# A table of places for the shared units of a decoder layer, a projection row one slot earlier, and the residual rows' fetches elsewhere in SP's queue

## The reference

```python
def attn(h):                                   # causal self attention
    q, k, v = split(h @ W_attn + b_attn, 3)    # to 16 heads
    q, k = _layernorm(q, q_gamma, q_beta), _layernorm(k, k_gamma, k_beta)
    p = softmax(where(causal, q @ k.T * 32 ** -0.5, min))
    return (p @ v) @ W_proj + b_proj
def xattn(x, ctx):                             # cross attention, top 32 of 512 keys
    Q, K, V = x @ Wq.T + bq, ctx @ Wk.T + bk, ctx @ Wv.T + bv
    s, i = top_k(Q @ K.T / sqrt(32), 32)
    return (softmax(s) @ V[i]) @ Wo.T + bo
def ffn(x):                                    # width 2048, quantized
    gate = silu(_bitlinear(x, w_gate)); up = _bitlinear(x, w_up)
    return _bitlinear(gate * up, w_down)
x = x + attn(_layernorm(x))
x = x + xattn(_layernorm(x), ctx)
x = x + ffn(_layernorm(x))
```

## Time and profile before

| | us |
|---|---|
| median of three executions | 3904.87 (3895.12 to 3911.36) |
| the profiled execution | 3917.24 |
| its span | 3915.5 |
| busy in it: PE, DVE, ACT, POOL | 3310.2, 3220.0, 2451.7, 1917.9 |
| first cross slot starts, last cross slot starts | 490.7, 3749.1 |
| mean granted clock of PE | 0.867 |

### The profile page before, as it was taken

The page is one execution under the profiler, slowest core; times in us unless marked ns, Lnnn a source line. Parts: engine busy times, 40 slices in busy tenths (PEclk is TensorE's granted clock), DMA queues, the critical chain, the costliest instruction groups (busy, mean ns, idle before and its releaser), DMA issues.

```text
span 3915.5 us, 61337 instructions
## 1 busy us (share of the span) xinstructions
PE 3310.2 (85%) x18502; PEld 2433.7 (62%) x18502; DVE 3220.0 (82%) x7571; ACT 2451.7 (63%) x4921; POOL 1917.9 (49%) x2444
## 2 busy tenths in 40 slices
PE   1577888999989998999999989999899988877765
PEld 1355567766666676667667667667666766554542
DVE  4311189999989999899989998999989998999961
ACT  2344466676777677667766677767666776555533
POOL 0122334446555466546654655546554654355445
PEclk7677878898999989988989999988998898887768
DMA  8112232232223222322223222322233221211100
GB/s 279 46 49 65 80 84 73 74 82 75 51 76 88 75 69 79 84 79 74 76 72 84 75 52 74 87 76 67 79 88 83 65 71 41 62 46 36 33 22 19
DMA packets 167443, 283.04 MB, mean 72 GB/s; under 512 B 40639, under 2 KB 52939, under 8 KB 166606
## 3 DMA queue, kind: packets, MB, share of 16 engines
q1 hardware_dynamic: 160782, 275.98, 25.9%
q10 hardware_dynamic: 6336, 3.15, 0.3%
HBM read 113.27 MB, written 31.46 MB: 37 GB/s over the span
## 4 chain that ended last, share of the span: by engine, by line
DVE 33%; PE 32%; POOL 11%; issue 8%; ACT 6%; SPq 4%; DMA 1%; DVEq 0%; POOLq 0%; ACTq 0%
DVE cW L881 15%; DVE top L876 12%; PE bank L682 6%; PE bank L607 6%; PE bank L654 5%; SPq L513 4%; PE bank L593 3%; PE bank L670 2%; PE bank L701 2%; PE bank L635 2%; POOL hh L1111 2%; POOL srs L1147 2%; POOL hh L1115 2%; PE bank L694 2%; DVE smx L1013 2%
## 5 line engine op out<-in xcount | busy, mean ns | idle before, releaser
L881 DVE MATCH_REPLACE8 cW<-top,cW 128x512 f32<-128x512 f32 x1536 | 1026.3, 676 | 0.0
L876 DVE MAX8 top<-cW 128x8 f32<-128x512 f32 x1536 | 980.7, 680 | 0.0
L1168 POOL TENSOR_TENSOR cS<-cS,cW 128x512 f32<-128x512 f32 x512 | 642.2, 1276 | 233.2 <-ACT cW L825 232.7
L797 ACT ACTIVATE PT<-bank 128x512 f32<-128x512 f32 (+3 forms) x1024 | 538.0, 525 | 314.4 <-PE bank L593 310.6
L607 PE MATMUL bank<-cv,PT 128*128 128x33 f32 x4096 | 586.0, 290 | 121.8 <-ACT PT L797 120.6
L607 PEld LDWEIGHTS bank<-cv,PT 128*128 128x128 f32 x4096 | 555.0, 210 | 157.0 <-ACT PT L797 151.0
L1175 POOL TENSOR_SCALAR cnb<-top 128x2 f32<-128x2 f32 x256 | 49.3, 193 | 871.6 <-DVE top L876 857.9
L607 PEld LDWEIGHTS bank<-sv,PT 128*128 128x128 f32 x2560 | 398.7, 211 | 77.7 <-ACT PT L797 55.4
L825 ACT ACTIVATE cW<-cW,cnb 128x512 f32<-128x512 f32 x512 | 347.8, 734 | 127.6 <-DVE cW L881 127.2
L819 ACT ACTIVATE cS<-cS,cnb 128x512 f32<-128x512 f32 x512 | 380.1, 742 | 46.9 <-POOL cnb L1175 24.0
L682 PE MATMUL bank<-w_group,xT 128*128 128x384 f32 x1024 | 403.3, 541 | 0.0
(11 more groups left out here) (151 smaller groups left out, 6131.8 us busy)
## 6 DMA issues: line engine op xcount, KB each, us to landing
sk_stack<-part SPq DMA_DIRECT2D x512, 64.0 KB, 2.0
sq_stack<-part SPq DMA_DIRECT2D x512, 64.0 KB, 2.0
ck_stack<-part SPq DMA_DIRECT2D x512, 64.0 KB, 2.0
cq_stack<-part SPq DMA_DIRECT2D x512, 64.0 KB, 2.0
w_group<-wa_by_group SPq DMA_DIRECT2D x32, 768.0 KB, 4.8
w_group<-wc_by_group SPq DMA_DIRECT2D x32, 768.0 KB, 4.3
feed<-in_x SPq DMA_DIRECT2D x32, 256.0 KB, 3.0
feed<-in_ctx SPq DMA_DIRECT2D x32, 256.0 KB, 3.0
```

Of the source, the lines that this page charges most:

```text
L797: act.activation(PT[k][:, 0:n], turned_ps[k][:, 0:n], ACT.Copy).then_inc(turned_read, step("turned_read", label))
L876: dve.max(top8[:, j, r, :], src[:]).then_inc(topk, step("topk", (c, r, "max", j)))
L881: dve.match_replace(cW[j][:], top8[:, j, r, :], src[:], REPLACED).then_inc(topk, step("topk", (c, r, "replace", j)))
L1168: pool.tensor_tensor(cS[m % 2][j][:], cS[m % 2][j][:], cW[j][:], ALU.subtract).then_inc(cprob, step("cprob", (m, j)))
```

## The change

`schedule(b)` is a table for each batch b of the slots, counted from the batch's first cross slot, in which its shared units stand, in place of the rule "three slots a tile". `cross_rows` move from 15, 16, 17, 18 to 15, 17, 18, 19. The 16 chunks of the MLP's gate and up stand in 20 to 33, ten early and six late; `hT` in 22, 25, 30, 35 (places 6, 9, 14, 3) and `down`, now apart, in 23, 25, 30, 37 (places 7, 9, 14, 5). The last two batches keep three slots a tile, the last but one three slots later. `self_qkv` row 0 moves to cell 5 of the slot before (q = 3), row 1 from cell 3 to 2, row 2 from 6 to 5, row 3 from cell 1 to 3. `self_out` moves from cell 3 to 4 where q = 2, and DVE's `self_rows` behind ROUND_1 of the second half. POOL's `inner_quant` also follows an early last chunk. On SP the residual rows' DMAs move from ahead of the weights and copies of a slot to behind them, and the fetches of `x1res`, `x2res` and `xres` are those of the next slot.

```diff
+def schedule(b):
+
+    def dense(first):
+        chunks = [(first + 3 * t + r, early) for t in range(NT) for r in range(2) for early in (True, False)]
+        ends = tuple(first + 3 * t + 2 for t in range(NT))
+        return chunks, ends, ends
+    if b == NB - 1:
+        return ((15, 16, 17, 18), *dense(17))
+    if b == NB - 2:
+        return ((15, 17, 18, 19), *dense(20))
+    chunks = [(20, True), (20, False), (21, True), (21, False), (22, False), (23, True), (24, True), (24, False),
+              (25, False), (26, True), (27, True), (29, True), (31, True), (32, True), (32, False), (33, True)]
+    return (15, 17, 18, 19), chunks, (22, 25, 30, 35), (23, 25, 30, 36 if b == NB - 3 else 37)
+
+
+def planned(s, part, entry, tiles=NT):
+
+    out = []
+    for b in range(NB):
+        for i, at in enumerate(schedule(b)[part]):
+            if at == entry(s - LAG - SLOTS * b):
+                out.append(tiles * b + i)
+    return out
+
+
 def cross_tile(s):
-    return tile_at(s, LAG + 15)
+    return next(iter(planned(s, 0, lambda at: at)), None)
 
 
 def x2_tile(s):
-    return tile_at(s, LAG + 16)
+    return cross_tile(s - 1)
...
 def mlp_chunk(s, early):
 
-    t, r = mlp_step(s)
-    return [(t, 2 * r + (not early))] if t is not None and r < 2 else []
+    return [divmod(i, NF) for i in planned(s, 1, lambda at: (at, early), NT * NF)]
+
+
+def mlp_inner(s):
+    return planned(s, 2, lambda at: at)
 
 
 def mlp_down(s):
-    t, r = mlp_step(s)
-    return [t] if t is not None and r == 2 else []
+    return planned(s, 3, lambda at: at)
 
 
 def cells(s):
 
     u = [[] for _ in range(CELLS)]
-    g, q = self_group(s), s % NT
+    q = s % NT
+    g = s // NT + 2
+    if q == 3 and 0 <= g < NGROUPS:
+        u[5].append(("self_qkv", g, 0))
+    g = self_group(s)
     if g is not None:
-        for at, cell, unit in ((0, 0, ("self_qkv", g, 0)), (0, 3, ("self_qkv", g, 1)), (0, 6, ("self_qkv", g, 2)),
-                               (1, 1, ("self_qkv", g, 3)), (3, 2, ("self_kT", g)), (3, 3, ("self_qT", g))):
+        for at, cell, unit in ((0, 2, ("self_qkv", g, 1)), (0, 5, ("self_qkv", g, 2)),
+                               (1, 3, ("self_qkv", g, 3)), (3, 2, ("self_kT", g)), (3, 3, ("self_qT", g))):
             if at == q:
                 u[cell].append(unit)
...
     if self_tile(s) is not None:
         u[2].append(("self_oT", self_tile(s)))
-        u[3].append(("self_out", self_tile(s)))
+        u[4 if q == 2 else 3].append(("self_out", self_tile(s)))
     if x2_tile(s) is not None:
         u[4].append(("x2T", x2_tile(s)))
+    for t in mlp_inner(s):
+        for n in range(NF):
+            u[3 + n].append(("hT", t, n))
     for early, cell in ((True, 2), (False, 6)):
         for t, n in mlp_chunk(s, early):
             u[cell] += [("gate", t, n), ("up", t, n)]
     for t in mlp_down(s):
-        for n in range(NF):
-            u[3 + n].append(("hT", t, n))
         u[7].append(("down", t))
     for k, f in enumerate(feeds(s)):
         u[5 + k].append(("feed", *f))
...
-                for t in mlp_down(s - 1):
-                    C.plan("h_dve", ("out", t))
                 for early, at in ((False, s - 1), (True, s)):
+                    for t in mlp_down(s - 1) if early else ():
+                        C.plan("h_dve", ("out", t))
...
                         done += len(feeds(s - 1))
                         while pending and ring[pending[0]] - RING < done:
                             load_feed(pending.pop(0))
-                        t = x1_tile(s)
-                        if t is not None:
-                            sp.wait_ge(x1_stats, upto("x1_stats", ("x1", t)))
-                            sp.dma_start(rows(x1_rows, t), xres[:]).then_inc(x1_out, step("x1_out", t, 16))
-                        t = x2_tile(s)
-                        if t is not None:
-                            sp.wait_ge(dve_rows, upto("dve_rows", ("x2", t)))
-                            sp.dma_start(rows(x2_rows, t), x2t[:]).then_inc(x2_out, step("x2_out", t, 16))
-                        t = cross_tile(s)
-                        if t is not None:
-                            if t:
-                                sp.wait_ge(dve_rows, upto("dve_rows", ("x2", t - 1)))
-                            sp.wait_ge(x1_out, upto("x1_out", t, 16))
-                            sp.dma_start(x1res[:], rows(x1_rows, t)).then_inc(x1res_in, step("x1res_in", t, 16))
-                        t = self_tile(s)
-                        if t is not None:
-                            if t:
-                                sp.wait_ge(x1_out, upto("x1_out", t - 1, 16))
-                                sp.wait_ge(x1_norm, upto("x1_norm", (t - 1, 4)))
-                            sp.dma_start(xres[:], rows(x_rows, t)).then_inc(xres_in, step("xres_in", t, 16))
-                        for t in mlp_down(s):
-                            sp.wait_ge(x2_out, upto("x2_out", t, 16))
-                            if t:
-                                sp.wait_ge(y_out, upto("y_out", t - 1, 16))
-                            sp.dma_start(x2res[:], rows(x2_rows, t)).then_inc(x2res_in, step("x2res_in", t, 16))
                         for at, which, g, before in loads:
                             if at == s:
                                 load_weights(which, g, before)
@@ -554,8 +554,33 @@
                             for unit, j in ((k_unit, 0), (k_unit, 1), (q_unit, 0), (q_unit, 1),
                                             (k_unit, 2), (q_unit, 2), (k_unit, 3), (q_unit, 3)):
                                 copy_part(unit, j)
+                        t = cross_tile(s)
+                        if t is not None:
+                            sp.wait_ge(dve_rows, upto("dve_rows", ("x2", t)))
+                            sp.dma_start(rows(x2_rows, t), x2t[:]).then_inc(x2_out, step("x2_out", t, 16))
+                        t = cross_tile(s + 1)
+                        if t is not None:
+                            if t:
+                                sp.wait_ge(dve_rows, upto("dve_rows", ("x2", t - 1)))
+                            sp.wait_ge(x1_out, upto("x1_out", t, 16))
+                            sp.dma_start(x1res[:], rows(x1_rows, t)).then_inc(x1res_in, step("x1res_in", t, 16))
+                        t = self_tile(s)
+                        if t is not None:
+                            sp.wait_ge(x1_stats, upto("x1_stats", ("x1", t)))
+                            sp.dma_start(rows(x1_rows, t), xres[:]).then_inc(x1_out, step("x1_out", t, 16))
                         for t in mlp_down(s - 1):
                             store_y(t)
+                        for t in mlp_down(s + 1):
+                            sp.wait_ge(x2_out, upto("x2_out", t, 16))
+                            if t:
+                                sp.wait_ge(y_out, upto("y_out", t - 1, 16))
+                            sp.dma_start(x2res[:], rows(x2_rows, t)).then_inc(x2res_in, step("x2res_in", t, 16))
+                        t = self_tile(s + 1)
+                        if t is not None:
+                            if t:
+                                sp.wait_ge(x1_out, upto("x1_out", t - 1, 16))
+                                sp.wait_ge(x1_norm, upto("x1_norm", (t - 1, 4)))
+                            sp.dma_start(xres[:], rows(x_rows, t)).then_inc(xres_in, step("xres_in", t, 16))
...
                         top(c, 0, ROUND_3)
                         top(c, 1, FIRST_MAX)
                         self_maxima(s, 0)
+                        top(c, 1, ROUND_1)
                         self_rows(s)
-                        top(c, 1, ROUND_1)
                         feed_stats_of(s + 1)
                         top(c, 1, ROUND_2)
                         mlp(s, True)
...
                     def inner_quant(s):
-                        for t, n in mlp_chunk(s, False):
+                        for t, n in mlp_chunk(s, True) + mlp_chunk(s, False):
                             if n == NF - 1:
```

More of the change, by code:

```diff
@@ L99, in cross_group @@
     return g if 0 <= g < NGROUPS else None
-def mlp_step(s):
-    b, at = divmod(s - (LAG + 17), SLOTS)
-    t, r = divmod(at, 3)
-    return (NT * b + t, r) if 0 <= b < NB and t < NT else (None, None)
 def mlp_chunk(s, early):
-    t, r = mlp_step(s)
-    return [(t, 2 * r + (not early))] if t is not None and r < 2 else []
+    return [divmod(i, NF) for i in planned(s, 1, lambda at: (at, early), NT * NF)]
+def mlp_inner(s):
+    return planned(s, 2, lambda at: at)
 def mlp_down(s):
-    t, r = mlp_step(s)
-    return [t] if t is not None and r == 2 else []
+    return planned(s, 3, lambda at: at)
 def cells(s):
     u = [[] for _ in range(CELLS)]
-    g, q = self_group(s), s % NT
+    q = s % NT
[3 more added lines that the diff above has]
+    g = self_group(s)
     if g is not None:
-        for at, cell, unit in ((0, 0, ("self_qkv", g, 0)), (0, 3, ("self_qkv", g, 1)), (0, 6, ("self_qkv", g, 2)),
```

(3 more changed lines are left out.)

## The result

The changed kernel took 3968.45 us (median of four, 3959.18 to 3971.99) against 3905.38 for the kernel before on the same chip: ratio 1.016 [1.013, 1.019], 63 us slower where I had forecast 40 faster.

A forecast was written before the change was run, and what follows sets the result against it. DVE and PE were both near full, so only DVE's idle time could return: -4.4 us a batch, six times -26, with -14 before the cross units, total -40, giving a median of 3865 us; range 3805 to 3925.

The forecast's parts named there:

- the early part: Before the cross units start: row 0 fills PE's 4.16 us wait for the copies; -3.6 us a group, four groups, -14.
- place 12: Batch place losing a projection row, `down` and four hT units, over 8 us of PE work; DVE's idle time put at 0.5.
- place 13: Batch place where PE, now early, waits for DVE's norms before `self_oT`; DVE's idle time put at 1.5, from 3.5.
- The weight load of q = 1: Places 1 and 5: row 3 in cell 3 delays the load for `cross_v`; PE waits 2.1 us, DVE pays 0.
- my other bound: Places 1 and 5: upper bound on DVE's cost from the late weight load, 3 us each, against 0 taken.
- Place 9: The wait for POOL's quantized `hh` covers PE's wait for the q = 1 weight load; idle time put at 1.0.
- the sum for place 10: Idle 8.8 + 1.4 + 1.8 - 2.5, less 2, gives 7.5; 5.5 once place 9's POOL wait and half clock fall away.
- The residual rows: Fetches a slot ahead but behind the copies: `x1res` comes no earlier in place 15, whose idle time goes 2.7 to 4.0.
- 3 by its fetch: Place 3 had no own term, being among eight places going 6.2 to 3.6; the prediction's wording is "0 by its fetch".
- Place 7's load: `w_group` lands near 2362.7 for row 0 in cell 5; PE waits 9 us, place 8 goes from 0.6 to 7.3.
- the first rival: Load not exposed: `w_group` lands before PE asks, or PE is late anyway; place 8 keeps 0.6; 3836 us, chance 0.26.
- the last rival: Half clock behind the gaps: place 8 waits 12, places 1 and 5 cost 3 each; 3929 us, chance 0.15.

## Why the prediction was wrong

Of the gains that the steps named, three came: the early part 18.0 us (predicted 14), place 12 at 0.3, place 13 at 1.5. PE waits for the load in places 7, 1 and 5. The terms below were wrong; together they are the 15.1 us a batch between 24.9 and 40.0.

*The weight load of q = 1 (the step that failed).* I had PE wait 2.1 us in places 1 and 5, and put DVE's cost at 0 since "PE's load in both slots is 3 us under DVE's". The wait was 3.0 and 2.4 us on average. The cost is not the wait but what stands behind it: `cross_v` took 8.3 us for its four eights of matmuls instead of 4.6, and what PE had in hand was spent. Place 2 paid 4.8 us more than I said; leaving out the load took it to 0.2. Even my other bound, 3 each, was short of place 2. I had the engines' loads about right (PE 20.55 us busy in place 1 against DVE's 24.74), and that was no cover. Nor does the length of the wait give the price: the 2.4 us in place 5 cost DVE only some 0.5 us, in place 6 (1.1 against 0.6 with the row in cell 1). Why place 5 is so cheap was not tested.

*Place 9, in the same step.* I wrote that there the wait for POOL covers the load. The runs show the reverse: that the row leaves cell 1 opens a gap of 1.14 us, the row runs at half clock and releases the load later, and both meet in place 10 (the run with the row in cell 2 parts the two). It idled 10.9 us, not 5.5, and 36 of the 58 us vanish when row 3 is back in cell 1 at places 9 and 13 alone. In the sum for place 10 I had counted the fall of the wait for POOL as a gain, to 5.5; with row 3 back in cell 1 the place idles 5.3, so that part of the sum holds.

*The residual rows.* I saw the fetch behind the copies and priced it in place 15 only (4.0; it was 6.2). The same order at place 3, a tile that the table itself puts there, I gave 0 ("3 by its fetch"). It idled 4.4 us, and 7.1 in the run with row 3 in cell 1, where PE was not late. Here the prediction missed the largest gain as well: the two DMAs ahead of the copies are worth 50 us by the ratios with the old rows.

*Place 7's load.* I said PE waits 9 us and place 8 takes 7.3; it waited 3.8 in the row above, and place 8 idled 3.0. Its load landed 7.8 us after its issue at most, but the row was reached late, at 2808.1, for PE had waited 3.86 us a batch for ACT in front of it: the first rival's argument. Place 7 itself stayed at 4.5 us where I took 1.2. The run with the table alone has 3.8 there, 3.4 of it DVE's maxima waiting for POOL's product `hh`: I put it down to the late chunk that the table sets in place 6, and didn't test it.

So the last rival came true in kind, half clock behind the gaps, at places 1 and 9, hardly at 5; place 8, where it put 12 us, idled 3.0. It gave 3929 where 3968 was measured, since it had neither place 9 nor place 3. The trace had its sign already in the earlier trace rows: a gap of 2.85 us and 0.50 behind it. The Trainium skill's section "HAM oscillation — how this bites in real kernels" of "TensorE: Matmul & The Clock Gate" says that PE is re-throttled by a wait for a DMA and that the work behind each such wait starts cold. The trace agrees in kind (2.08 against 1.16 us for eight matmuls, 5.38 against 2.85 for a row), but its gaps, 2.98 and 1.14 us, are shorter than the waits of 3 to 5 us that the section describes, and behind the shorter one two rows of the run with the row in cell 2 stayed at full clock.

## What to carry to other kernels

A transfer into a single buffer is released by its last reader: when that reader moves by a few us, check that the load still lands before the next reader, in every place where the pattern recurs and with the reader's duration at half clock. What a wait of PE costs is the wait and the slower matmuls behind it, so spare time on PE of the size of the wait isn't cover. A DMA that a row needs soon doesn't belong behind a block of copies in the same queue. And a part of a schedule is worth judging again when its surroundings have changed: the same table was 19 us slower alone and 37 faster in the kernel whose two DMAs, rows and `self_out` had been set right.

## What the runs showed of the hardware

The eight matmuls of a projection row took 2.85 us with the row in cell 1 of place 9, and 5.38 or 4.54 us in cell 3 in two kernels shown above, behind a gap of 1.14 us for ACT. I had not expected so short a gap to matter. In cell 2, behind the same gap, it took 4.45 to 4.54 us in three batches and 2.85 in two: the length of the gap alone doesn't decide. Gaps of 0.30 and 0.62 us in place 10 of the changed kernel stood in a stretch with a mean clock of 1.00. What lets the clock fall behind one gap and not behind another stays open.
